# Layer 0's maxima by four Pool transfers, outputs three units later, and another order of routing and of layer 1's opening

## The reference

```
x += L0 cross-attention: 32 query heads of 16, 8 key heads, softmax(QK/4) V, Wo, biases
x += L0 mixture of experts: sigmoid gate, top 4 of 16 experts, silu(g)*u, plus a shared expert
x += L1 cross-attention: 32 heads of 128, 4 key heads, keys = [context, latents] (256 keys per tile)
x += L1 linear with routed low-rank adapters (top 2 of 8)
```

## Time and profile before

| | |
|---|---|
| median of 3 runs | 1342.53 us (1341.86 to 1344.42) |
| the profiled execution | 1342.44 us |
| its span | 1341.1 us |
| mean granted PE clock | 0.963 of full |
| PE, DVE, ACT, POOL busy | 91%, 63%, 52%, 29% |
| layer 0 attention | 0 to 251 us |
| routing and shared expert | 252 to 310 us |
| 47 expert tiles | 310 to 558 us |
| layer 1's opening | 558 to 622 us |
| layer 1's attention and adapters | 622 to 1341 us |

### The profile page before, as it was taken

The page is one execution under the profiler, slowest core; times in us unless marked ns, Lnnn a source line. Parts: engine busy times, 40 slices in busy tenths (PEclk is TensorE's granted clock), DMA queues, the critical chain, the costliest instruction groups (busy, mean ns, idle before and its releaser), DMA issues.

```text
span 1341.1 us, 16367 instructions
## 1 busy us (share of the span) xinstructions
PE 1218.0 (91%) x5860; PEld 951.4 (71%) x5860; DVE 839.9 (63%) x1549; ACT 690.7 (52%) x1575; POOL 389.7 (29%) x452
## 2 busy tenths in 40 slices
PE   4939877797999999878999999999999999999997
PEld 4725554465667667556888888887788888888865
DVE  5526665676777667555466666676456666667857
ACT  3315445415777777523555555565345555556621
POOL 5310001014777768300223233232012232232300
PEclk8969988898999999879999999999999999999999
DMA  7553413119766975552022122121221221211101
GB/s 246 157 168 75 123 28 143 63 41 359 173 104 148 276 205 101 110 173 71 24 64 63 56 64 60 59 64 48 55 64 58 61 63 41 63 57 47 62 1 63
DMA packets 73664, 130.74 MB, mean 97 GB/s; under 512 B 11024, under 2 KB 30352, under 8 KB 70992
## 3 DMA queue, kind: packets, MB, share of 16 engines
q1 hardware_dynamic: 56288, 81.44, 19.6%
q0 software_dynamic: 17296, 48.26, 14.5%
HBM read 150.63 MB, written 29.36 MB: 134 GB/s over the span
## 4 chain that ended last, share of the span: by engine, by line
PE 70%; DVE 9%; POOL 6%; issue 5%; DMA 5%; ACT 3%; SPq 1%; POOLq 0%; ACTq 0%; DVEq 0%
PE bank L451 53%; PE bank L1914 6%; PE bank L1890 4%; POOL moe L1537 3%; PE bank L644 3%; POOL xs L1526 2%; PE bank L631 1%; DMA xs<-xn_rows,token_in 1%; SPq L491 1%; DMA wf_raw<-in_wffn,weight_row 1%; DMA m_rows<-m0T 1%; POOL wf_raw L1516 1%; PE bank L616 1%; DVE xn L422 1%; PE bank L1214 1%
## 5 line engine op out<-in xcount | busy, mean ns | idle before, releaser
L1882 POOL TENSOR_SCALAR p<-p,mx 128x256 f32<-128x256 f32 x256 | 163.2, 654 | 533.4 <-DVE mx L1876 533.4
L1123 DVE TENSOR_TENSOR wf_lo<-wf_raw,wf_hi 128x512 fp32r<-128x512 f32 x192 | 124.4, 689 | 41.4 <-ACT wf_hi L1117 36.0
L451 PE MATMUL bank<-xnA_hi,w1q_hi 128*128 128x512 f32 x288 | 118.5, 412 | 7.2 <-DVE w1q_lo L1701 3.8
L1868 ACT ACTIVATE p<-bank,mx 128x256 f32<-128x256 f32 x256 | 118.0, 485 | 10.7 <-DVE mx L1858 10.6
L1117 ACT ACTIVATE wf_hi<-wf_raw 128x512 fp32r<-128x512 f32 x192 | 110.1, 625 | 15.2 <-DMA wf_raw<-in_wffn,weight_row 14.3
L451 PE MATMUL bank<-xnA_hi,w1q_lo 128*128 128x512 f32 x288 | 114.7, 398 | 0.0
L451 PE MATMUL bank<-xnA_lo,w1q_hi 128*128 128x512 f32 x288 | 114.2, 396 | 0.0
L1897 ACT ACTIVATE p1T_hi<-bank 128x512 fp32r<-128x512 f32 x128 | 75.1, 596 | 65.7 <-PE bank L1890 65.7
L1822 ACT ACTIVATE q1T_hi<-bank 128x512 fp32r<-128x512 f32 x64 | 38.2, 597 | 132.8 <-PE bank L451 132.8
L451 PE MATMUL bank<-w1o_hi,a1T_hi 128*128 128x512 f32 x256 | 105.2, 411 | 0.1
L1828 DVE TENSOR_TENSOR q1T_lo<-bank,q1T_hi 128x512 fp32r<-128x512 f32 x64 | 44.2, 691 | 94.8 <-ACT q1T_hi L1822 94.8
(11 more groups left out here) (337 smaller groups left out, 3153.2 us busy)
## 6 DMA issues: line engine op xcount, KB each, us to landing
w_raw<-in_wq SPq DMA_DIRECT2D x64, 256.0 KB
w_raw<-in_wo SPq DMA_DIRECT2D x64, 256.0 KB
q0st<-q_rows SPq DMA_DIRECT2D x8, 768.0 KB, 5.6
moe<-xn SPq DMA_DIRECT2D x2, 2304.0 KB, 10.5
q_rows<-q0T_hi SPq DMA_DIRECT2D x16, 256.0 KB
returned<-moe SPq DMA_DIRECT2D x8, 512.0 KB, 7.5
k0bd<-k_rows SPq DMA_DIRECT2D x16, 192.0 KB, 5.9
x<-in_x SPq DMA_DIRECT2D x8, 256.0 KB, 6.7
```

Source lines behind the costliest of these rows:

```text
L451: ins = nc.tensor.matmul(ps, a, b, start=(n == 0), stop=(n == len(pairs) - 1))
L1123: nc.vector.tensor_tensor(wf[m % 2][1][:, a, c, :], raw[m % STREAMS][:, a, c, :], wf[m % 2][0][:, a, c, :].bitcast(F32), ALU.subtract).the ...
L1868: ins = nc.scalar.activation(pr1[s % 2][:, h, :], banks.of(("s1", s, n))[:, hh * 2 * P:(hh + 1) * 2 * P], ACT.Exp, bias=m[:, UH + h:UH + h ...
L1882: ins = nc.gpsimd.tensor_scalar(pr1[s % 2][:, h, :], pr1[s % 2][:, h, :], m[:, 3 * UH + h:3 * UH + h + 1], 1.0, ALU.mult, ALU.mult)
```

## The change

1. Maxima. m_rows and SP's `maxima` are gone. Pool issues four transfers per batch from m0T straight into q0st, each 16 rows of 128 values into one partition; turned_scores wait for all four. Pool's order: maxima 0 and 1 after the output bias, then for each later batch the value spread and the maxima. ACT's reuse of m0T waits for them.

```diff
-            def maxima(b):
-                sp.wait_ge(S["m0_lo"], b + 1)
-                load(m_rows[b].rearrange("q r t -> r q t"), mT[b % 2][:, :, :].bitcast(F32)).then_inc(S["st_m"], 16)
-                sp.wait_ge(S["st_m"], 16 * (b + 1))
-                load(qst[b % RING0][QROWS:QROWS + MROWS, :, :, :].bitcast(F32).rearrange("p k j t -> p (k j t)"),
-                     m_rows[b].rearrange("q (h r) t -> (q h) (r t)", h=2)).then_inc(S[f"ld_m0{b % RING0}"], 16)
...
+            def maxima(b):
+                pool.wait_ge(S["m0_lo"], b + 1)
+                half = H0 // 2
+                for q in range(2):
+                    for h in range(2):
+                        row = QROWS + 2 * q + h
+                        nc.gpsimd.dma_start(
+                            qst[b % RING0][row:row + 1, :, :, :].bitcast(F32).rearrange("p k j t -> p (k j) t"),
+                            mT[b % 2][h * half:(h + 1) * half, q, :].bitcast(F32)).then_inc(S[f"ld_m0{b % RING0}"], 16)
...
+            maxima(0)
+            maxima(1)
+            for b in range(2, B):
                 values_spread(b)
-            pool.wait_ge(S["k0_mm"], 2)
-            pool.wait_ge(S["v0_mm"], B)
-            nc.gpsimd.memset(zeros, 0.0).then_inc(S["vp_set"], 1)
...
+                maxima(b)
+                if b == HB:
+                    pool.wait_ge(S["k0_mm"], 2)
+                    pool.wait_ge(S["v0_mm"], B)
+                    nc.gpsimd.memset(zeros, 0.0).then_inc(S["vp_set"], 1)
```

```diff
-        LAG_Y = 6
+        LAG_Y = 9
```

```diff
+        def gpsimd_tile_share():
             hot = tile_hot[:, :, :, :].bitcast(F32)
...
+            for n, (c, part) in enumerate(((1, share_hi), (2, share_lo))):
+                pool.wait_ge(S["tile_hot"], 2 * n + 1)
+                nc.gpsimd.tensor_tensor(
+                    tile_hot[:, :, c, :], hot[:, :, 2, :],
+                    flat(part).bitcast(F32).unsqueeze(2).broadcast_to([P, PAIRS, TILE_COLS]),
+                    ALU.mult).then_inc(S["tile_hot"], 1)
...
             vector_z(3)
+            vector_weight_rows()
             vector_shares()
             vector_tile_token()
...
             vector_z(5)
-            vector_tile_share()
             vector_row_hot()
-            vector_weight_rows()
...
             weights(2)
+            gpsimd_tile_share()
...
+            pool.wait_ge(S["gate_mm"], 2)
+            pool.wait_ge(S["gu_mm"], B)
             weights(4)
```

```diff
-        WEIGHTS_AT = {TILES - 3: 2, TILES - 2: 2, TILES - 1: KT}
+        WEIGHTS_AT = {j: 1 for j in range(TILES - 2 * KT - 1, TILES - 1)}
...
-        FIRST_LOADS = 2 * KT + 3
+        FIRST_LOADS = 3 * KT
...
+            sp.wait_ge(S["st_moe1"], 16 * adds_before(TILES, 1))
+            for q in range(B // 4):
+                bring(1, q, S[f"returned{q}"])
+            sp.wait_ge(S["st_moe0"], 16 * adds_before(TILES, 0))
+            for q in range(B // 4):
+                bring(0, q, S[f"rows_in{q}"])
+            for q in range(B // 4, B // 2):
+                for s in (1, 0):
+                    bring(s, q, S[f"rows_in{q}"])
...
             if ring == "out" and slot < 4:
-                for s in range(2):
-                    act.wait_ge(S[f"st_moe{s}"], 16 * adds_before(TILES, s))
+                act.wait_ge(S["dn_mm"], FFN_STEPS)
...
+        def tensor_first_opening():
+            for m in range(1, KV1):
+                tensor_keys(0, m, score_banks)
             for b in range(HB):
...
+                tensor_values(0, 0, b, score_banks)
+            for j in range(3, 7):
+                tensor_norm(4, j, out_banks)
+            for m in range(KV1, 2 * KV1):
+                tensor_keys(0, m, score_banks)
...
+        def vector_first_opening():
+            for _ in range(3):
+                vector_weight()
+            vector_keys(0, 0)
+            vector_keys(0, 1)
+            vector_weight()
+            for b in range(HB):
+                vector_return(b, 1)
+            vector_keys(0, 2)
+            vector_keys(0, 3)
+            for j in range(2):
+                vector_return(2 * j, 0)
+                vector_return(2 * j + 1, 0)
+                vector_norm(4, j)
+            vector_norm(4, 2)
+            for b in range(HB):
+                vector_norm(4, b + 3)
+                vector_values(0, 0, b)
+            for m in range(KV1, 2 * KV1):
+                vector_keys(0, m)
+                vector_weight()
+                for s in (1, 0):
+                    vector_return(HB + m - KV1, s)
```

More of the change, by code:

```diff
@@ L807, in keys @@
             def keys(half):
-                dve.wait_ge(S["k0_hi"], half + 1)
+                dve.wait_ge(S["k_hi"], half + 1)
                 nc.vector.scalar_tensor_tensor(
@@ L1058, in sync_experts, with bring @@
                 sync_weight(k)
[L1059 to L1066 removed]
+            def bring(s, q, sem):
+                load(returned[s][:, 2 * q:2 * q + 2, :],
+                     moe[s].rearrange("(n p) d -> p n d", p=P)[:, 2 * q:2 * q + 2, :]).then_inc(sem, 16)
+            sp.wait_ge(S["st_moe1"], 16 * adds_before(TILES, 1))
[7 more added lines that the diff above has]
+                    bring(s, q, S[f"rows_in{q}"])
         def tensor_gate(h, n):
@@ L1579, in gpsimd_experts, with vector_return, returned_all @@
                     weights(i + STREAMS)
-        def vector_return(b):
-            dve.wait_ge(S[f"rows_in{b // 2}"], 48)
-            dve.wait_ge(S["shared_add"], b + 1)
-            vstep.step(nc.vector.tensor_tensor(x[:, b, :], returned[0][:, b, :], x[:, b, :], ALU.add))
-            nc.vector.tensor_tensor(x[:, b, :], returned[1][:, b, :], x[:, b, :], ALU.add).then_inc(S["moe_add"], 1)
+        def vector_return(b, s):
+            q = b // 2
+            if b >= HB:
+                dve.wait_ge(S[f"rows_in{q}"], 48)
+            elif s:
+                dve.wait_ge(S[f"returned{q}"], 16)
+            else:
+                dve.wait_ge(S[f"rows_in{q}"], 32)
+            if s:
+                dve.wait_ge(S["shared_add"], b + 1)
+            else:
+                dve.wait_ge(S["moe_add"], b + 1 if b < HB else 2 * b + 1)
+            nc.vector.tensor_tensor(x[:, b, :], returned[s][:, b, :], x[:, b, :], ALU.add).then_inc(S["moe_add"], 1)
+        def returned_all(b):
+            return S["moe_add"], HB + b + 1 if b < HB else 2 * (b + 1)
         def norm_x_ready(g, k):
@@ L1661, in sync_attention1 @@
         def sync_attention1():
-            for k in range(FIRST_LOADS + 1, len(stream)):
+            for k in range(FIRST_LOADS, len(stream)):
                 sync_weight(k)
@@ new lines, in scalar_first_opening @@
+        def scalar_first_opening():
+            for _ in range(3):
+                scalar_weight()
+            scalar_keys(0, 0)
+            scalar_keys(0, 1)
+            scalar_weight()
+            scalar_keys(0, 2)
+            scalar_keys(0, 3)
+            scalar_values(0, 0, 0)
+            scalar_values(0, 0, 1)
+            scalar_norm(4, 1)
+            scalar_values(0, 0, 2)
+            scalar_values(0, 0, 3)
+            for j in range(3, 7):
+                scalar_norm(4, j)
+            for m in range(KV1, 2 * KV1):
+                scalar_keys(0, m)
+                scalar_weight()
@@ L1945, in vector_out @@
             else:
-                dve.wait_ge(S["moe_add"], half * HB + b + 1)
+                dve.wait_ge(*returned_all(tile))
             nc.vector.tensor_tensor(x[:, tile, :], banks.of(("y1", s))[:, :], x[:, tile, :],
@@ L1953, in half_steps @@
         def half_steps(half, values, query, weight, steps, norm, last, ending):
-            for b in range(HB):
+            for b in range(HB if half else 0):
                 weight()
-                if half:
-                    values(0, b)
+                values(0, b)
             for n in range(UH):
@@ L1991, in steps @@
                     tensor_attend(s - 1)
-            first_opening(nothing, lambda h, m: tensor_keys(h, m, score_banks) if m else None,
-                          lambda part, b: tensor_values(0, part, b, score_banks), nothing,
-                          lambda g, j: tensor_norm(g, j, out_banks))
+            tensor_first_opening()
             for half in range(2):
@@ L2020, in steps @@
                     scalar_attend(s - 1)
-            first_opening(scalar_weight, scalar_keys, lambda part, b: scalar_values(0, part, b), nothing, scalar_norm)
+            scalar_first_opening()
             for half in range(2):
```

68 lines of the change are left out of this document (22 added, 46 removed).

## The result

The changed kernel took 1294.9 us in the median of 4 runs (1289.6 to 1297.2), the kernel before 1342.2 (4 runs); the ratio is 0.964, 95% interval 0.961 to 0.968. A second comparison, of five runs, gave 1292.4 us and 0.962 [0.961, 0.964]. The profiled execution took 1297.2 us with a span of 1295.9: 45.2 us less than the span before.

A forecast was written before the change was run, and what follows sets the result against it. PE, busy for 91% of the span, was taken as the bound, so only its idle or low-clock time could be won: 13.9 + 8.6 + 3 + 19 = 44.5 us off 1342.4 gave 1298 us, range 1276 to 1317.

The forecast's parts named there:

- Part 1: First batch's maxima: four Pool transfers replace two SP transfers, so PE goes on at 82.4 instead of 96.3: 13.9 us gained.
- A: Rival on Pool's maxima chain: t is 1.26 us like the gathers, every batch waits 3 us: 1308 us; chance 0.27.
- B: Rival on Pool's maxima chain: t is 0.35 us like SP's, chain 3.7 us, no wait: 1275 us; chance 0.16.
- t: Issue and gap of one Pool transfer of maxima: taken as 0.95 us, between bounds of 0.26 and 1.26.
- Part 2: Layer 0's loop: outputs nine units behind instead of six remove the a0T_lo wait, maxima are late next: 8.6 us gained.
- 23.9 us: Loop: seven batches each pay 3.4 us, 1.8 of wait for the maxima and 1.6 of low clock.
- 122.5 us: Loop stage without waits for maxima: PE's work of 111.5 us, 2 of low clock at the start, and the tail.
- Part 3: Routing: earlier weight loads end the wait for gathered tokens, share products go to Pool: 3 us gained, ends -3 and +6.
- Part 4: Layer 1's opening: keys 0 right behind the last gate_up, values ahead of keys 4: 19 us gained, ends 14 and 22.
- C: Rival on Pool's maxima transfers: DVE holds up Pool's issue, t is 2.7 us, slower at 1354 us; chance 0.03.
- D: Rival on routing: it loses 3 us instead of gaining 3, as the lock falls the wrong way: 1304 us; chance 0.06.
- 75 - 32t: Whole kernel's gain for t above about 0.9: 17.7 - 4t from the first maxima, 35 - 28t in the loop, 22 elsewhere.

The follow-up runs named there:

- e6_first_clear: The changed kernel with SP holding the 12 stores of the second half's queries until the first batch's maxima have landed: 1295.8 us, ratio 0.965.
- r2_sp_maxima: The changed kernel with the maxima sent by SP over DRAM again, as before the change: 1300.3 us, ratio 0.968.
- r3_lag6: The changed kernel with outputs six units behind again (LAG_Y 6 instead of 9): 1305.2 us, ratio 0.972.
- e9_eight_clear: The changed kernel with each Pool transfer of maxima cut in two and SP's bulk transfers in the loop held until the maxima landed: 1304.6 us, ratio 0.972.
- r4_routing_old: The changed kernel with the share products on DVE and the weight rows behind row_hot again: 1299.7 us, ratio 0.968.
- e7_eight: The changed kernel with each of Pool's four transfers of maxima cut into two of 4 KB, eight per batch: 1333.3 us, ratio 0.992.

## Why the prediction was right, and which of its terms were not

**The total, 1298.0 us**, lay 3.1 us over the measured 1294.9, and the sum of gains, 44.5 us, against 45.2 between the two spans. It lies well inside the range, 1276 to 1317. That the sum is so close is luck: in part 1 and in the loop an error each way cancels. Three of the prediction's own signs of being wrong came: no wait for the maxima in two of the seven later batches and 0.25 us in two more, a tail of 13.9 us and not 12, and keys 4 later than 32 us after keys 0. The range was added up wrongly too: A's 1308 with the lower ends of parts 1, 3 and 4 (6.7, 6 and 5 us) gives 1325 and not 1317, and B's 1275 lies outside it.

**Part 1 (13.9 forecast, 13.4 measured).** The four transfers took 2.25 us, not 3.8, for t is 0.48 and not 0.95; the landing took 5.49, not 3. The two errors, 1.6 and 2.5 us, nearly cancel. I took the gather as the nearer row and it was not: the truth lay in the lower quarter of the bounds 0.26 and 1.26, nearer to SP's row. e6_first_clear shows that the landing is contention with SP's stores (1.68 us without them), and r2_sp_maxima that nearly all of the gain is leaving SP's queue (20.3 against 8.4 us from the ready maxima on).

**Part 2 (8.6 forecast, 13.0 measured) is where the steps failed**, in both directions. That the wait for a0T_lo goes with LAG_Y 9 and that the maxima are next, with a slack of 4.24 us, held: r3_lag6 lost 12.8 us, and at a chain of 0.75 + 1.91 + 1.7 = 4.4 us the wait was 0.25, near what that slack gives; e9_eight_clear at 0.75 + 4.08 + 1.6 = 6.4 us waited 2.3. Wrong was the size, 1.8 + 1.6 us in each of seven batches: with t at 0.48 it was 0.25 or less and no low clock wherever nothing collided (1.2 us in the last batch). So the 23.9 us were really about 7, and these 7 came from something the prediction did not have: two landings beside SP's bulk transfers. Rival B (no wait) had this term right. But its other term, 122.5 us for the stage without these waits, was too small by some 12: a batch takes 15.1 us and not 8 x 1.34 + 2.8 + 0.25 = 13.8. In the batch from 112.5 us two units take 1.98 and 1.91 us in place of 1.34, behind waits of 0.24 for the maxima and 0.35 for exp, which the prediction named and took as covered; what the rest of the 1.3 us is the profile does not show. In the last batch the turns of the norm wait 3.6 us in four places, which the prediction did not have, and from the last unit to the end of the last projection it took 18.4 us where I had 12.2 and a projection. Hence B's 1275 was not reached either.

**Part 3 (3 forecast, 5.2 measured).** The direction of the lock was as taken, one behind the other, but a Pool product costs 2.63 us and not 3.8, for two of them the missing 2.3 us. Counted in PE's waits, 5.83 and 1.07 us for gathered tokens went and the tokens' matmuls came 1.7 us later. r4_routing_old gives back exactly the 5.2 us.

**Part 4 (19 forecast, 17.8 measured).** Keys 0 without a wait and no longer tile period held. Keys 4 came at +34.9 us, not +32.2: the last scatter-add took 6.77 us to land (4.85 before) and the rows 6.71 (5.2 before), 3.4 us together. Layer 1's weight loads move at the same time and may be why; that was not tried. Of the parts, the spread of the weights is shown (8.0 us), the early first array is worth nothing measurable, and the order with the values ahead of keys 4 was not tried alone. Undone one at a time, the maxima's way, the later outputs, the routing and the spread weights cost 7.9, 12.8, 7.2 and 8.0 us, together 35.9 of the 51 us between the kernels; whether the rest lies in the other orders of the opening, or in what the parts do for one another, is not shown.

**The rivals.** A, B and C all turned on t, and t was 0.48. For C, neither the lock nor Pool's descriptors behind DVE show: 32 transfers beside a DVE busy for about 11 of 15 us took 484 ns in the median and 750 at most. The Trainium skill (SBUF — State Buffer, SBUF: two separate sides) warns of 2-port modes keeping Pool from its descriptors; no run here shows that. D did not happen. The terms behind the formula 75 - 32t, a wait for what the chain is too long and about 1.6 us of low clock behind it, are nearly right where SP is held back: in e9_eight_clear 2.2 us of Pool give 2.0 of wait and 1.3 of clock a batch. Without that the step of e7_eight comes as soon as Pool's last transfer starts behind SP's bulk, here beyond some 2 us of issue; rival C's price had no such step in it and would probably have been too low, which no run tried.

**Left open:** the 2.6 us before the first maxima, in code that the change does not touch (the granted clock up to 75 us is 0.86 after and 0.91 before), what Pool's pause in the fifth batch is, and 2.1 us in the rest of layer 1, of which 1.4 are a longer wait in front of the last adapters (2.7 against 1.3 us).

## What to carry to other kernels

A small transfer on which the next stage waits is priced by its queue and by what moves beside it, not by its hops: take it off a queue that is full of stores, and let the queue that issues the bulk wait for its landing. Look at when the bulk is issued relative to the small transfer: here a last transfer that started 0.1 us behind the bulk landed 2 us later than one that started 0.2 us ahead of it, and so a small delay turned a slope into a step. When moving a bulk transfer out of the way, find the next reader on that queue first; held-back stores cost more at their new place than at the old one, twice.

## What the hardware showed unexpectedly

Pool's transfer without indices took 484 ns for 8 KB and 518 ns for 4 KB, back to back, where the gather of 128 rows takes 967 ns and 0.30 us of gap: halving the bytes saved nothing, what counted was the number of transfers. An 8 KB transfer landed in 1.7 us on quiet engines and in 3.8 to 6.3 us beside hundreds of KB that SP had issued, though it is on another queue; the Trainium skill (DMA: Bandwidth & Descriptors, Queues, rings and completion order) says that an engine takes turns between the queues a packet at a time. The trace of e7_eight agrees: the last 4 KB transfer of the sixth batch, issued at 186.84 behind the zeros of 185.33, landed at 193.10, ahead of both stores of zeros (196.7 and 202.4). The seventh batch of the changed kernel can't tell, for its maxima landed at 173.99, just behind the last zeros at 173.3. In the fifth batch Pool stood still for 0.32 us between two such transfers, in each of the ten traces in which it sends four per batch; what it waited for the profile does not show.
